# Values four key tiles behind the scores, a seventh probability buffer, and fourteen half tiles in one run

## The reference, cut to what matters

```python
xn = group_norm(x, gn_weight, gn_bias)
qkv = jnp.einsum('oc,bchw->bohw', qkv_weight, xn) + qkv_bias[None, :, None, None]
attn = jnp.einsum('bhdk,bhdq->bhkq', q, k) / np.sqrt(hd).astype(np.float32)
attn = jax.nn.softmax(attn, axis=-1)
out = jnp.einsum('bhkq,bhdq->bhdk', attn, v).reshape(b, c, h, w)
out = jnp.einsum('oc,bchw->bohw', proj_weight, out) + proj_bias[None, :, None, None]
x = x + out
...
out = conv3x3(relu(batch_norm(x, gamma0, beta0)), quantize_w1bit(w0))
out = conv3x3(relu(batch_norm(out, gamma1, beta1)), quantize_w1bit(w1))
return out + x
```

## Time and profile before

| | us |
|---|---|
| median of 3 runs | 2740.03 |
| the runs | 2738.54 to 2740.18 |
| the profiled execution, its own time | 2736.51 |
| its span, first to last instruction | 2734.5 |
| PE busy in the span | 2613.4 (96%) |
| DVE busy | 2144.9 (78%) |
| POOL busy | 2055.0 (75%) |
| ACT busy | 1661.6 (61%) |

### The profile page before, as it was taken

The page is one execution under the profiler, slowest core; times in us unless marked ns, Lnnn a source line. Parts: engine busy times, 40 slices in busy tenths (PEclk is TensorE's granted clock), DMA queues, the critical chain, the costliest instruction groups (busy, mean ns, idle before and its releaser), DMA issues. The chain is left out here.

```text
span 2734.5 us, 73082 instructions
## 1 busy us (share of the span) xinstructions
PE 2613.4 (96%) x31180; PEld 1171.3 (43%) x31180; DVE 2144.9 (78%) x2768; ACT 1661.6 (61%) x2597; POOL 2055.0 (75%) x1164
## 2 busy tenths in 40 slices
PE   4999999999999999999999999999999999799898
PEld 2444444435444444344444444454444444344343
DVE  7788888748888888577888887588888884788785
ACT  4666666766666667646666667666666666244432
POOL 2799999987999999857999999879999998000022
PEclk9999999999999999999999999999999999999999
DMA  5100000002000000041000000010000000521022
GB/s 222 60 2 2 2 2 2 2 2 69 2 2 2 2 2 2 2 156 54 2 2 2 2 2 2 2 32 2 2 2 2 2 2 2 192 69 47 31 92 92
DMA packets 26940, 80.17 MB, mean 29 GB/s; under 512 B 1920, under 2 KB 2176, under 8 KB 25600
## 3 DMA queue, kind: packets, MB, share of 16 engines
q1 hardware_dynamic: 25648, 73.01, 7.6%
q10 hardware_dynamic: 976, 2.63, 0.3%
HBM read 58.86 MB, written 16.78 MB: 28 GB/s over the span
## 5 line engine op out<-in xcount | busy, mean ns | idle before, releaser
L615 POOL TENSOR_TENSOR acc_pool<-acc_pool,prob 128x512 f32<-128x512 f32 (+1 forms) x960 | 1749.2, 1822 | 158.1 <-ACT prob L681 30.5
L681 ACT ACTIVATE prob<-ps,exp_scale 128x512 f32<-128x512 f32 x2048 | 1297.6, 684 | 675.4 <-PE ps L912 672.1
L1005 DVE TENSOR_REDUCE m_part<-ps 128x2 f32<-128x1024 f32 x1024 | 1248.1, 1225 | 312.2 <-PE ps L868 225.9
L894 PE MATMUL ps<-prob,vals 64*64 64x512 f32 x8192 | 1049.3, 590 | 0.0
L906 PE MATMUL ps<-q_hi,k_hi 64*64 64x512 f16 x4096 | 398.1, 378 | 8.1 <-ACT prob L681 6.2
L906 PE MATMUL ps<-q_lo,k_hi 64*64 64x512 f16 x4096 | 397.0, 376 | 0.0
L912 PE MATMUL ps<-m_rows,shift 64*64 64x512 f16 x4096 | 397.0, 376 | 0.0
L906 PE MATMUL ps<-q_hi,k_lo 64*64 64x512 f16 x4096 | 397.0, 376 | 0.0
L1098 DVE TENSOR_TENSOR ps<-ps,prob 128x512 f32<-128x512 f32 x452 | 312.6, 692 | 85.2 <-ACT prob L681 85.1
L894 PEld LDWEIGHTS ps<-prob,vals 64*64 64x64 f32 x8192 | 293.1, 133 | 185.7 <-issue 23.4
L906 PEld LDWEIGHTS ps<-q_hi,k_hi 64*64 64x64 f16 x4096 | 116.5, 104 | 576.7 <-ACT prob L681 520.6
(11 more groups left out here) (134 smaller groups left out, 1679.1 us busy)
## 6 DMA issues: line engine op xcount, KB each, us to landing
xt<-in_x SPq DMA_DIRECT2D x32, 512.0 KB, 4.5
xf<-in_x SPq DMA_DIRECT2D x4, 2048.0 KB, 16.1
xn<-in_x SPq DMA_DIRECT2D x16, 512.0 KB, 7.7
x_scratch<-y_tile SPq DMA_DIRECT2D x16, 512.0 KB, 5.4
rows<-x_scratch SPq DMA_DIRECT2D x8, 576.0 KB, 5.1
rows<-x_scratch SPq DMA_DIRECT2D x8, 544.0 KB, 4.6
xt<-x_scratch SPq DMA_DIRECT2D x4, 1024.0 KB, 5.2
y_tile<-x_scratch SPq DMA_DIRECT2D x4, 1024.0 KB, 5.2
```

Of the source, the lines that this page charges most:

```text
L615: nc.gpsimd.tensor_tensor(acc[:, part], acc[:, part], tile[:, part], ALU.add).then_inc(pool_add, 1)
L681: nc.scalar.activation(prob[:, n % PBUF, h * TB:(h + 1) * TB], g.ps[:, score_bank(it, kt, h)], ACT.Exp, scale=g.exp_scale[:]).then_inc(exp ...
L894: last = mm(into[own[h], :], vals[keys, kt, own[h]], prob[keys, n % PBUF, h * TB:(h + 1) * TB], start=(kt == 0), stop=(kt == KT - 1))
L1005: v.tensor_reduce(m_part[:, block % 2, :, u], source, AX.X, ALU.max).then_inc(mx_used, 1)
```

## The change

- `LAG` goes from 3 to 4, and with it `SUMS_AT`, `OUTPUT_AT` and `DIVIDE_AT`: values product, column sums, output copy, upper add and division all stand one key tile later.
- `PBUF` goes from 6 to 7.
- `DVE_HALVES` becomes the 14 tiles 13 to 26.
- `half_sum` is no longer a tensor of its own but a quarter of `y_tile` (slot 1, channel block 1). ACT's copy into it waits for the stores from that slot (`y_out`), and DVE's `residual` of slot 1 waits until POOL has added the half sum of the image's last block (`tot_ready`).
- The constant `mask` is stored with 4 columns instead of 512 and read with a repeat along the last axis by DVE in `write_max_rows` (L1055).

```diff
-PBUF = 6
+PBUF = 7
...
-NCONST = 2 * P + TB
+NCONST = 2 * P + QT
...
-LAG = 3
+LAG = 4
...
-DVE_HALVES = [12, 13, 14, 16, 17, 18, 20, 21, 22, 23, 24, 25, 26]
+DVE_HALVES = list(range(13, 27))
...
-    mask = g.const[:, MASK:MASK + TB].rearrange("p (a n) -> p a n", a=QT)
+    mask = g.const[:, MASK:MASK + QT].unsqueeze(2).to_broadcast([P, QT, P])
...
-        half_sum = sb("half_sum", [P, TB])
+        half_sum = g.y_tile[:, 1, CB - 1]
...
-                nc.gpsimd.tensor_tensor(acc[:, 0:TB], acc[:, 0:TB], half_sum[:], ALU.add).then_inc(tot_ready, 1)
+                nc.gpsimd.tensor_tensor(acc[:, 0:TB], acc[:, 0:TB], half_sum, ALU.add).then_inc(tot_ready, 1)
...
-                nc.scalar.activation(half_sum[:], acc_dve(it), ACT.Copy).then_inc(half_copied, 1)
+                act.wait_ge(g.y_out[1], 16 + 16 * (it // (2 * NB)) * (NB // 2))
+                nc.scalar.activation(half_sum, acc_dve(it), ACT.Copy).then_inc(half_copied, 1)
...
+                if s:
+                    dve.wait_ge(tot_ready, (b + 1) * 2 * NB)
...
-        c[[t, HD + t], MASK + t * P:MASK + (t + 1) * P] = 1.0
+        c[[t, HD + t], MASK + t] = 1.0
```

## The result

The changed kernel takes 2705.31 us (median; 2705.09 to 2705.33), the kernel before 2739.28 (2735.61 to 2740.18) on the same chip. The ratio is 0.9879, 95% interval 0.9867 to 0.9891: 34 us or 1.2% faster. The forecast was 2707.1. The profiled execution took 2705.33 us with a span of 2703.5, so spans differ by 31.0 us, medians by 34.0.

A forecast was written before the change was run, and what follows sets the result against it. POOL's additions were taken to bound the blocks, with PE waiting at the column sums. Profiled 2736.5 us less 32.7 and 3.3 plus 3.1 gives 2703.6; the 2740.0 median less 32.9 gives 2707.1 us, range 2702 to 2715.

The forecast's parts named there:

- POOL is the bound inside the blocks, and PE pays at L884: POOL's block cycle is 64.61 us, PE's 63.45; PE waits at the column sums (L884) 24 times, 31.3 us.
- POOL's cycle becomes 63.52: One full tile fewer and one half more per block saves POOL 1.09 us, level with PE's 63.45.
- All 24 waits go; room at the last boundary 1.4 us: At the column sums: first-boundary room 3.18 us, less 0.35 drift over five blocks and 1.42 at the last; gain 32.7 us.
- The later request is part of the gain: With one more tile of lag, the column sums ask for POOL's result 1.94 us later, counted into the boundary room.
- The slow clock goes, 3.3 us: Behind the last boundary of the first two pairs, PE's slow stretch of 1.67 us disappears with the long waits.
- The lag costs 3.1 us: One values product moves from each pair's head to its end: net 0.77 us a pair, 3.1 us in all.
- DVE costs nothing: A fourteenth half add of 0.69 us in 28 blocks fits DVE's run at PE's pitch, costing nothing.
- third rival: DVE becomes the bound in the run of fourteen half adds, losing 1.4 us in 28 blocks: 2746 us; chance 0.03.
- Buffers, half sum, mask, new waits: nothing: The seventh buffer, ACT's and DVE's new waits around the half sum, and the smaller mask were costed at nothing.
- (1): The last boundary of each pair still waits and the slow clock stays, 8.1 us in all: 2715 us; chance 0.07.
- (2): POOL's cycle doesn't shorten because it waits for ACT; only the later request counts: 2735.5 us; chance 0.04.
- (4): POOL and ACT hold each other through `prob`; only the seventh buffer acts, at most 2.8 us: 2740 us; chance 0.02.

The follow-up runs named there:

- Run 1: The kernel before with only the list of half tiles changed, to 13 to 26 in one run (lag 3, six buffers); 2704.84 us.
- run 7: The changed kernel with `m_neg` computed on ACT instead of DVE in all blocks but the first of a pair; 2703.62 us.
- run 8: The changed kernel with fifteen half tiles (12 to 26), lag 4 and seven buffers kept; 2702.78 us.
- run 3: The changed kernel with lag 3 and the old list of half tiles, leaving only seventh buffer, half sum and mask new; 2739.67 us.
- run 2: The changed kernel with the old list of half tiles and six buffers, so only the lag of four is new; 2731.47 us.
- run 5: The changed kernel with a lag of five tiles instead of four; 2708.10 us.
- run 9: The changed kernel with lag 3 and fifteen half tiles (12 to 26); 2699.30 us.
- run 12: The changed kernel with lag 2, half tiles 12 to 27, the half sum's copy one tile later, and `m_neg` on ACT; 2701.11 us.
- Run 11: The changed kernel with lag 2, sixteen half tiles (12 to 27) and the copy of the half sum one tile later; 2745.74 us.
- run 6: The changed kernel with six buffers instead of seven; 2704.98 us.
- run 10: The kernel before with only its list of half tiles changed, to 12 to 26 (lag 3, six buffers); 2699.39 us.

## Why the prediction was right, step by step

- **POOL is the bound inside the blocks, and PE pays at L884.** Right. Run 1 changes nothing but POOL's and DVE's shares and takes the whole gain.
- **POOL's cycle becomes 63.52.** Right: 63.50 to 63.55 in the first and third pair; every second cycle of the second and fourth is 0.27 longer. These longer ones were there before (64.88 beside 64.60) and stay in run 7, so `m_neg` doesn't make them; their cause stays open.
- **All 24 waits go; room at the last boundary 1.4 us.** Right: none is left, and the room is 1.07 to 1.53 us. But two parts of the sum were off and cancelled. At the first boundary the room is 167.81 - 165.03 = 2.78, not 3.18. The drift of 0.07 a block, 0.35 in all, didn't happen (2.99 at the second boundary, 485.57 - 482.58 = 2.99 at the sixth), because PE was held at POOL's pace. In run 7, where it isn't, the drift is there: 2.77 to 2.45. The prediction also named, as a sign, some idle time of POOL ended by ACT. In the changed kernel only the first block of a pair has more of it (0.36 us in the first pair); the blocks in the middle of a pair get it with fifteen half tiles (1.3 us a block in run 8).
- **The later request is part of the gain.** That was the sum's way of counting it, and the runs show it was not needed: the faster POOL alone covers six of seven boundaries, and the last costs 0.3 to 0.7 us. The new lag buys that and costs as much.
- **The slow clock goes, 3.3 us.** Right in the trace: 1.00 where 0.81 stood. In run 3, where the waits stay, the stretch has 0.76, and in run 2, with waits of 1.0 us at most at these places, 1.00. The size was right too: from the last boundary's column sums to the next column sums pass 112.08 us in the first pair and 61.48 in the second before, and 110.47 and 59.84 in run 1, which has the same lag and a clock of 1.00 there. That is 1.61 + 1.64 = 3.25 us; the third and the fourth pair lose nothing.
- **The lag costs 3.1 us.** Right, measured as 2.8 to 3.1 in run 5 and as 3.5 between runs 8 and 9.
- **DVE costs nothing.** Half right. The run of fourteen half adds keeps PE's pitch, fifteen and sixteen too (the sixteen in run 12). The rule of the Trainium skill, "VectorE: DVE Perf Modes", section "The DRAIN you can't avoid", spoke against the change and would have given the third rival's time; no run shows the drift it stands for. Run 11's 2745.7 comes near that rival's 2746 by another way. But I looked only at the half adds. The failed step is the one that says that DVE's cover is untouched: POOL is now further ahead when `m_neg` comes, in the first full tile behind the halves (from 214.82 us, `m_neg` at 216.22) and no longer in the last half (from 214.93 us before, `m_neg` at 216.01), and that cost 3.1 us in PE's cycles.
- **Buffers, half sum, mask, new waits: nothing.** Right, by runs 3 and 6.
- **The sum.** 32.9 us expected between the spans, 31.0 measured. `m_neg` takes 3.1 in PE's cycles, of which run 7 got back 1.7 in its time. Of the remaining 1.2 us the other way, at most 0.3 is the lag's smaller price, and 0.4 a tile in the first block of each pair that was 2.05 us long before, behind an `m_neg` of 0.86, and is 1.94 now. The waits were larger than the 32.7 of the sum: the 24 cycles of PE that end with a wait before are together 33.4 us longer than the same cycles of run 9, which has the same lag and no such wait. That is 0.7 more. With these sizes 33.4 + 3.3 + 0.4 - 3.1, less 2.8 to 3.1 for the lag, gives 30.9 to 31.2 us. The median came out 1.8 us below the forecast although the profiled execution took 1.7 more than its share of it (2705.33 against 2703.6): I had added the 3.5 us by which the median of before stood over its profiled execution. The changed kernel has no such distance. That the forecast of the median came so close is in part luck: two errors of opposite sign.
- **The rivals.** The last boundary doesn't wait (1); POOL's cycle does shorten (2), and run 2 shows what this would have given, 2731.5 against my 2735.5, which had kept the slow clock; DVE isn't the bound in the run (3); buffers are not the matter (4), by run 3.

## What to carry to other kernels

When two engines share a reduction, shift work from the one that is late until it waits for its producer by itself; here one list of tile numbers gave all of the 39 us, and the longer lag and the extra buffers only looked needed. Then look at what the shift has done to the phase of everything else on the two engines: with lag 2 and one tile more the same move made the kernel slower than it was. When a wait has gone from the list, compare the block cycles of the two engines once more: if they still agree to some hundredths, the slower one still sets the pace somewhere. Look for small operations whose duration varies (0.17 to 1.99 us for the same 8 columns): that is a wait which no list of waits shows.

## What the runs showed of the hardware that I had not expected

- A scaling of 128x8 values from SBUF to SBUF on DVE takes 0.17 us when POOL is idle or less than 0.05 us from the end of an addition, and otherwise lasts until POOL's addition in progress ends: 0.98 (to 217.20, POOL to 217.18) in the changed kernel, 1.99 (to 220.03, POOL to 220.01) in run 11. It stands in the trace as busy time. On ACT the same operation takes 0.21 to 0.23 us at every phase that runs 7 and 12 show. DVE's reductions and half adds, which read at most one operand from SBUF, keep 1.21 to 1.23 and 0.64 to 0.70 us beside the same additions.
- So the price of that operation depends on the phase between two engines: from run 9 to run 11, with one tile more in the list, one tile of lag less and the copy of the half sum one tile later, it went from nothing to 1.87 us a block. Which of the three moved the phase was not separated. Run 12 takes 44.6 us from run 11 by moving it to ACT.
- The kernels in which PE waits for 2.2 us or more at the last boundary of a pair vary more from run to run (2735.6 to 2740.2 before, 2737.5 to 2741.6 in run 3) than those without such waits (2705.1 to 2705.3 after, 2699.3 to 2699.6 in run 10). The clock behind these waits is 0.81 and 0.76 there and 1.00 here. The profiled execution of before had the lower clock behind the last boundary of two pairs out of four, that of run 3 of three, at 1.6 us each. In the executions of the kernel before that were timed beside the experiments, those with a mean granted clock of 0.993 took 2734.7 to 2737.2 us, those with 0.990 or 0.991 2737.3 to 2741.4. So an execution's time may go with the number of pairs that lose the clock; no experiment was made on it.
